# Normalising attention probabilities before the value matmul, with v as the stationary operand

## What is computed

```
q = l2norm((xn @ w_q) per head) * q_scale;  k the same;  v = xn @ w_v
k, v = concat(null_k, k), concat(null_v, v)             # 2 null keys and 256 keys
sim  = 8 * q @ k.T + distance * slope, causal
attn = softmax(sim, axis=-1)
out  = (attn @ v) gathered over the heads @ w_out
```

## Time and profile before

| | us |
|---|---|
| runs | 723.68, 727.42, 747.17; median 727.42 |
| profiled execution | 723.42, its span 721.6 |
| PE / DVE / ACT / POOL busy | 594.1 / 409.7 / 435.5 / 319.5 |
| granted TensorE clock, mean | 0.904 of full speed |

### The profile page before, as it was taken

How to read it: one execution, slowest core, us unless ns; L and a number is a source line. 1 busy time by engine, 2 the same in 40 slices (tenths; PEclk the granted TensorE clock), 3 DMA queues, 4 the chain that set the end, 5 groups by cost and what they waited for, 6 DMA issues and landing times.

```text
span 721.6 us, 12802 instructions
## 1 busy us (share of the span) xinstructions
PE 594.1 (82%) x3695; PEld 465.9 (65%) x3695; DVE 409.7 (57%) x1540; ACT 435.5 (60%) x1184; POOL 319.5 (44%) x281
## 2 busy tenths in 40 slices
PE   2467499914167689898999899999999999999997
PEld 2456388802046468566677667867787787777675
DVE  7546165523346463688446466647655764765574
ACT  1745466502156456766757587678768776876652
POOL 4477700035566632234677724404421441335770
PEclk9999699966577599979959999999999999999789
DMA  9611223241001000010111000000000000000220
GB/s 330 226 49 44 74 74 94 62 145 29 15 16 29 16 1 0 17 43 1 34 44 48 10 12 24 23 24 23 24 23 23 23 23 23 24 13 12 74 76 24
DMA packets 33074, 33.72 MB, mean 47 GB/s; under 512 B 4512, under 2 KB 28992, under 8 KB 32240
## 3 DMA queue, kind: packets, MB, share of 16 engines
q1 hardware_dynamic: 28912, 24.52, 10.8%
q0 software_dynamic: 4096, 8.40, 4.0%
HBM read 19.85 MB, written 13.04 MB: 46 GB/s over the span
## 4 chain that ended last, share of the span: by engine, by line
PE 43%; POOL 12%; DVE 9%; issue 5%; ACT 3%; DMA 1%; DVEq 0%; POOLq 0%; ACTq 0%
PE b_last L1737 8%; PE b_upB L1694 8%; PE b_rest L1718 4%; POOL sorted_rows L511 4%; POOL rn L570 3%; POOL taken L620 2%; PE b_upA L1656 2%; PE b_upB L1543 2%; PE b_upB L1682 2%; PE b_rest L1706 2%; PE b_upB L1577 2%; PE b_last L1388 2%; POOL qk L313 1%; PE b_rest L1682 1%; POOL taken L542 1%
## 5 line engine op out<-in xcount | busy, mean ns | idle before, releaser
L570 POOL TENSOR_TENSOR rn<-ss,halves 128x8 f32<-128x8 f32 x64 | 105.2, 1643 | 248.0 <-DVE ss L1264 240.0
L841 ACT ACTIVATE prb<-prb,mneg 128x130 f32<-128x130 f32 (+1 forms) x256 | 114.8, 449 | 73.5 <-DVE mneg L1331 72.0
L1331 DVE CUSTOM_DVE_ANT_0 prb<-b_upB,bias 128x130 f32<-128x130 f32 (+1 forms) x256 | 83.0, 357 | 92.1 <-PE b_upB L1694 90.8
L1737 PEld LDWEIGHTS b_last<-v,prT 128*128 128x128 f32 x768 | 106.7, 204 | 24.9 <-DVE qs_all L1319 12.2
L1737 PE MATMUL b_last<-v,prT 128*128 128x64 f32 x768 | 111.5, 284 | 9.0 <-DVE qs_all L1319 8.9
L1694 PE MATMUL b_upB<-qkT 64*128 64x258 f32 (+1 forms) x512 | 98.0, 412 | 6.6 <-DVE mneg L1331 4.7
L852 ACT ACTIVATE prT<-b_rest 128x512 f32<-128x512 f32 (+1 forms) x128 | 62.0, 484 | 33.1 <-PE b_rest L1718 30.2
L511 POOL DMA_INDIRECT sorted_rows<-xf_all,pos x64 | 66.0, 1031 | 27.5 <-issue 18.8
L1694 PEld LDWEIGHTS b_upB<-qkT 64*128 64x128 f32 x512 | 49.6, 206 | 37.6 <-issue 19.4
L1718 PE MATMUL b_rest<-cst,prb 128*128 128x128 f32 x384 | 69.4, 292 | 0.6 <-ACT prb L841 0.3
L776 ACT ACTIVATE sq<-qk 128x512 f32<-128x512 f32 x64 | 40.3, 630 | 43.3 <-DVE ss L1262 41.3
(11 more groups left out here) (301 smaller groups left out, 1301.2 us busy)
## 6 DMA issues: line engine op xcount, KB each, us to landing
moe_buf<-sorted_rows SPq DMA_DIRECT2D x20, 128.0 KB, 2.5
expert_rows<-moe_buf SPq DMA_DIRECT2D x20, 128.0 KB, 1.8
moe_buf<-sorted_rows SPq DMA_DIRECT2D x39, 64.0 KB, 1.9
expert_rows<-moe_buf SPq DMA_DIRECT2D x39, 64.0 KB, 1.5
sorted_rows<-v SPq DMA_DIRECT2D x2, 1024.0 KB, 6.8
bias<-w_up SPq DMA_DIRECT2D x1, 2048.0 KB, 13.2
down<-w_dn SPq DMA_DIRECT2D x2, 1024.0 KB, 9.1
moe_buf<-w_up SPq DMA_DIRECT2D x4, 512.0 KB, 3.8
```

The lines of the kernel that those rows point to most:

```text
L570: nc.gpsimd.tensor_tensor(rn[hs], ss[hs], halves[:], ALU.pow).then_inc(*pool_f1(f"root{n}"))
L841: nc.scalar.activation(prb[p % 3][:, i, 0:n], prb[p % 3][:, i, 0:n], ACT.Exp, scale=-1.0, bias=mneg[:, qt, h:h + 1], accum_out=lsum[:, qt, ...
L1331: nc.vector.tensor_tensor_reduce(prb[p % 3][:, i, 0:n], b_sim[i][:, 0:n], bias[:, h, KEYS - n:KEYS], 1.0, FMAX, ALU.add, ALU.min, mneg[:, ...
L1737: ins = nc.tensor.matmul(b_pv[:, at:at + DH1], prT[p3 % 3][:, i, c * P:(c + 1) * P], v[:, c, h * DH1:(h + 1) * DH1], start=(p3 % 4 == 0 an ...
```

## The change

The probabilities themselves are now normalised, on DVE, in `prb`: in each step two reciprocals (one instruction) and two multiplications of 130 or 258 columns, ahead of the copy of the null columns. `turned_values` turns them in step p-2 instead of p-1, behind the wait for this normalisation, and `values` follows four steps behind instead of three. There v is the stationary operand (64 columns) and `prT` the moving one (128 columns): head A writes partitions 0 to 63 of `b_pv`, head B partitions 64 to 127, and a half's values lie there already turned. The null part becomes four matmuls of 128 columns, one step later. DVE copies `b_pv` straight to `oT`, first in step 8, 12, 16 and 20. The product with the sums (`o_half`), the four turns of each half and the eight-wide reciprocal go.

```diff
--- before.py
+++ after.py
@@ -335,22 +335,20 @@
             out += [f"op{h}" for h in outputs_at(p)] + [f"simB{p}"] * (p < STEPS)
-            out += [f"oT{h}" for h in halves_at(p, 8)]
-            out += [f"pv{p - 3}"] * (3 <= p < STEPS + 3)
-            out += [f"pvn{h}" for h in halves_at(p, 6)]
-            return out + [f"prT{p - 1}"] * (1 <= p <= STEPS)
+            out += [f"pv{p - 4}"] * (4 <= p < STEPS + 4)
+            out += [f"pvn{h}" for h in halves_at(p, 7)]
+            return out + [f"prT{p - 2}"] * (2 <= p < STEPS + 2)
         def dve_head_steps(p):
-            out = [x for h in halves_at(p, 7) for x in (f"rl{h}", f"norm{h}")]
+            out = [f"oT{h}" for h in halves_at(p, 8)]
             if p < STEPS:
...
             out += [x for h in halves_at(p, 5) for x in (f"pnh{h}", f"pnT{h}")] + [f"add{h}" for h in outputs_at(p)]
-            out += [f"null{p - 1}"] * (1 <= p <= STEPS)
-            return out + [f"oT{h}" for h in halves_at(p, 8)]
+            return out + [x for x in (f"rl{p - 1}", f"norm{p - 1}", f"null{p - 1}") if 1 <= p <= STEPS]
...
             out = [f"exp{ab}{p}" for ab in "AB"] if p < STEPS else []
-            return out + [f"prT{p - 1}"] * (1 <= p <= STEPS)
+            return out + [f"prT{p - 2}"] * (2 <= p < STEPS + 2)
@@ -843,14 +841,14 @@
             def values(b, p):
-                if 1 <= p <= STEPS:
-                    p1 = p - 1
-                    n1 = P * (p1 // HP + 1)
...
+                if 2 <= p < STEPS + 2:
+                    p2 = p - 2
+                    n2 = P * (p2 // HP + 1)
...
@@ -1307,17 +1305,11 @@
                 n = NULL + P * (qt + 1)
-                for half in halves_at(p, 7):
-                    tile, first = half // 2, half % 2 * HALF
-                    dve.wait_ge(*act_heads.at(b, f"expB{4 * half + 3}"))
-                    heads8 = rl[:, tile, first:first + HALF]
-                    nc.vector.reciprocal(heads8, lsum[:, tile, first:first + HALF]).then_inc(*dve_heads(f"rl{half}"))
-                    dve.wait_ge(*dve_heads.at(b, f"rl{half}"))
+                for half in halves_at(p, 8):
                     dve.wait_ge(*pe_heads.at(b, f"pvn{half}"))
-                    dve.wait_ge(*(pe_heads.at(b, f"oT{half - 2}") if half >= 2 else pe_heads.at(b - 1, f"oT{half + 2}")))
-                    nc.vector.tensor_tensor(o_half[half % 2].rearrange("p (h d) -> p h d", h=HALF), b_pv.rearrange("p (h d) -> p h d", h=HALF),
-                                            heads8.unsqueeze(2).to_broadcast([P, HALF, DH1]), ALU.mult).then_inc(*dve_heads(f"norm{half}"))
+                    dve.wait_ge(*(pe_heads.at(b, f"op{half - 1}") if half else pe_heads.at(b - 1, f"op{STEPS // 4 - 1}")))
+                    nc.vector.tensor_copy(oT[:].rearrange("p a q -> p (a q)"), b_pv).then_inc(*dve_heads(f"oT{half}"))
                 if p < STEPS:
@@ -1354,7 +1346,15 @@
                     half, at = p1 // 4, p1 % 4 * 2 * NULL
+                    q1, h1, n1 = p1 // HP, 2 * (p1 % HP), NULL + P * (p1 // HP + 1)
                     dve.wait_ge(*act_heads.at(b, f"expB{p1}"))
+                    nc.vector.reciprocal(rl[:, q1, h1:h1 + 2], lsum[:, q1, h1:h1 + 2]).then_inc(*dve_heads(f"rl{p1}"))
+                    dve.wait_ge(*dve_heads.at(b, f"rl{p1}"))
+                    for i in range(2):
+                        part = prb[p1 % 3][:, i, 0:n1]
+                        ins = nc.vector.tensor_scalar(part, part, rl[:, q1, h1 + i:h1 + i + 1], None, ALU.mult)
+                    ins.then_inc(*dve_heads(f"norm{p1}"))
+                    dve.wait_ge(*dve_heads.at(b, f"norm{p1}"))
                     if half >= 2:
@@ -1363,11 +1363,6 @@
                                           prb[p1 % 3][:, :, 0:NULL].unsqueeze(1).to_broadcast([P, 3, 2, NULL])).then_inc(*dve_heads(f"null{p1}"))
-                for half in halves_at(p, 8):
-                    dve.wait_ge(*pe_heads.at(b, f"oT{half}"))
-                    dve.wait_ge(*(pe_heads.at(b, f"op{half - 1}") if half else pe_heads.at(b - 1, f"op{STEPS // 4 - 1}")))
-                    nc.vector.tensor_copy(oT[:].rearrange("p a q -> p (a q)"), b_turned[half]).then_inc(*dve_heads(f"oT{half}"))
@@ -1609,8 +1604,6 @@
                     pe.wait_ge(tile_loaded[i % 4], 16 * (i // 4 + 1))
-                    for half in halves_at(p - 1, 8):
-                        pe.wait_ge(*dve_heads.at(b, f"oT{half}"))
@@ -1664,7 +1657,7 @@
                     pe.wait_ge(*dve_heads.at(b, f"null{4 * half + 3}"))
-                    pe.wait_ge(*(dve_heads.at(b, f"simA{p - 1}") if p <= STEPS else act_heads.at(b, f"prT{STEPS - 1}")))
+                    pe.wait_ge(*(dve_heads.at(b, f"simA{p - 1}") if p <= STEPS else act_heads.at(b, f"prT{STEPS - 2}")))
                     nc.tensor.transpose(b_null[half], pn3[half % 2][:], ident).then_inc(*pe_heads(f"pnT{half}"))
@@ -1676,8 +1669,8 @@
                             pe.wait_ge(*dve_heads.at(b, f"simB{p - 1}"))
-                        elif half == 2:
-                            pe.wait_ge(*dve_heads.at(b, "pnT3"))
+                        else:
+                            pe.wait_ge(*(act_heads.at(b, f"prT{STEPS - 1}") if half == 2 else dve_heads.at(b, "add2")))
@@ -1693,58 +1686,48 @@
-                for half in halves_at(p, 8):
-                    pe.wait_ge(*dve_heads.at(b, f"norm{half}"))
-                    if p < ROUND - 2:
-                        pe.wait_ge(*(dve_heads.at(b, f"oT{half - 1}") if half else dve_heads.at(b - 1, "oT2")))
-                        for i in tile_at(b, p - 1, 0):
-                            pe.wait_ge(tile_dve["xl"], i + 1)
-                    else:
-                        pe.wait_ge(*dve_heads.at(b, "add2"))
-                    for i in range(4):
-                        ins = nc.tensor.transpose(b_turned[half][:, i * P:(i + 1) * P], o_half[half % 2][:, i * P:(i + 1) * P], ident)
-                    ins.then_inc(*pe_heads(f"oT{half}"))
             def turned_values(b, p):
-                if 1 <= p <= STEPS:
-                    p1 = p - 1
-                    nc1 = p1 // HP + 1
-                    pe.wait_ge(*(act_heads.at(b, f"prT{p1 - 1}") if p1 else dve_heads.at(b - 1, "add3")))
-                    pe.wait_ge(*act_heads.at(b, f"expB{p1}"))
+                if 2 <= p < STEPS + 2:
+                    p2 = p - 2
+                    nc2 = p2 // HP + 1
+                    pe.wait_ge(*(act_heads.at(b, f"prT{p2 - 1}") if p2 else dve_heads.at(b - 1, "add3")))
+                    pe.wait_ge(*dve_heads.at(b, f"norm{p2}"))
+                    if p2 == STEPS - 1:
+                        pe.wait_ge(*dve_heads.at(b, "pnT3"))
                     for i in range(2):
...
             def values(b, p):
-                if 3 <= p < STEPS + 3:
-                    p3 = p - 3
-                    q3 = p3 // HP
-                    if p3 % 4 == 0:
-                        pe.wait_ge(*(dve_heads.at(b, f"norm{p3 // 4 - 1}") if p3 else dve_heads.at(b - 1, f"norm{STEPS // 4 - 1}")))
-                    if p3 == 0:
+                if 4 <= p < STEPS + 4:
+                    p4 = p - 4
+                    if p4 % 4 == 0:
+                        pe.wait_ge(*(dve_heads.at(b, f"oT{p4 // 4 - 1}") if p4 else dve_heads.at(b - 1, f"oT{STEPS // 4 - 1}")))
+                    if p4 == 0:
                         pe.wait_ge(*act_f1.at(b, "v3"))
-                    pe.wait_ge(*act_heads.at(b, f"prT{p3}"))
-                    for i in range(2):
-                        h = 2 * (p3 % HP) + i
-                        at = (p3 % 4 * 2 + i) * DH1
-                        for c in range(q3 + 1):
-                            ins = nc.tensor.matmul(b_pv[:, at:at + DH1], prT[p3 % 3][:, i, c * P:(c + 1) * P], v[:, c, h * DH1:(h + 1) * DH1],
-                                                   start=(p3 % 4 == 0 and i == 0 and c == 0), stop=False, skip_group_check=True)
-                    ins.then_inc(*pe_heads(f"pv{p3}"))
-                for half in halves_at(p, 6):
+                    pe.wait_ge(*act_heads.at(b, f"prT{p4}"))
+                    at = p4 % 4 * P
+                    for c in range(p4 // HP + 1):
+                        for i in range(2):
+                            h = 2 * (p4 % HP) + i
+                            ins = nc.tensor.matmul(b_pv[i * DH1:(i + 1) * DH1, at:at + P], v[:, c, h * DH1:(h + 1) * DH1],
+                                                   prT[p4 % 3][:, i, c * P:(c + 1) * P], start=(p4 % 4 == 0 and c == 0),
+                                                   stop=False, skip_group_check=True)
+                    ins.then_inc(*pe_heads(f"pv{p4}"))
+                for half in halves_at(p, 7):
                     if b == 0 and half == 0:
...
                     pe.wait_ge(*dve_heads.at(b, f"pnT{half}"))
-                    nc.tensor.matmul(b_pv, pnT[:], nvbd[:, half % 2], start=False, stop=True, skip_group_check=True)\
-                        .then_inc(*pe_heads(f"pvn{half}"))
+                    for i in range(4):
```

(3 more changed lines are left out.)

18 lines of the change are left out of this document (9 added, 9 removed).

## The result

The changed kernel took 793.07 us (median of 4 runs, 788.40 to 796.42) against 726.25 us for the kernel before (4 runs): a ratio of 1.093, interval 1.083 to 1.102. The forecast was 750 us, its range 718 to 772. The direction was right, the size was 2.5 times too small (66 us lost between the profiled executions, where 27 were forecast), and the time lies outside the range.

What follows compares the result with a forecast made beforehand. The prediction took PE to be the bound (busy 64.89 of 65.80 us in the sixth round) and summed 723.4 - 14 - 6 + 11 + 29 + 7 = 750 us, range 718 to 772.

Steps and rivals of the forecast that it cites:

- The turns, the values and the null part: On PE: dropped turns -14 us, values with two heads side by side -6, null part in four matmuls +11.
- The rival in which column pairs need nothing around them: Groups of values on PE cost their passes alone, 130 columns under 0.27 us; 700 us in all, chance 0.09.
- The wait for the copy: PE's first values of a half wait for DVE's copy to oT at steps 8, 12, 16: +29 us.
- The failed step: DVE normalisation, 0.75 or 0.87 us a step: free while DVE idles, but moves its lag.
- Rounds without tiles: Part of the wait for the copy to oT: +8 us in three rounds, +1 in the last.
- Column halves that do not run together: Both heads write the same bank, so values groups take 0.64 and 1.07 us; about 783 us, chance 0.06.
- slow multiplications: DVE's normalising multiplications at their slow end, about 0.25 us more a step; 762 us, chance 0.08.
- The rival of waits half as long: Waits half as long and pairs a little cheaper, so no change: 728 us, chance 0.27.
- The waits near the end of a round: Product with w_out and ACT's first copy of v wait, 0.4 and 0.5 us each: +7 us, between 0 and 14.

Runs made afterwards that it cites:

- no_norm: Changed kernel without the normalisation's reciprocals and multiplications, timetable kept (turns at two steps, values at four): 743.8 us, ratio 1.021 to the kernel before.
- the added turns: Changed kernel plus unread identity turns on PE in rounds 0, 1, 7 (two: 1.085) or 0, 1, 2, 7 (two: 1.057; four: 1.067), ratios to the kernel before.
- early_no_norm: Changed kernel without the normalisation, in the timetable of the kernel before (turns at one step, values at three): ratio 0.968 to the kernel before.
- values_early_no_norm: Changed kernel without the normalisation, turns kept at two steps, values at three and the copy to oT a step earlier: 775 and 759 us in two runs.
- sums_spread: early_no_norm plus reciprocals of eight sums, spread to 512 columns by a DVE copy, turned on PE, multiplied on the way to oT: ratio 0.988 to the kernel before.

## Why the prediction was wrong

The sign and the mechanism it named were right, the size was not.

- **The turns, the values and the null part** (-14, -6, +11). Together -9, or -1.1 us a round; measured -2.0 (65.8 to 63.8). Column halves run together (as the row halves of the earlier trace rows do) and their groups are shorter than forecast, by 0.06 and 0.05 us; the null part cost 0.18 instead of 0.34. The rival in which column pairs need nothing around them did not hold: 0.37 is over its 0.27. The Trainium skill (TensorEngine Tiling (Array Packing), Performance Considerations) recommends the swap for up to twice the speed; the groups of 0.40 and 0.84 us became 0.37 and 0.59, a gain of 8% and 30%.
- **The wait for the copy** (+29). Forecast about 20 places with 20 to 30 us; measured 20 with 24.1. But 8.9 us of such waits stood in the kernel before, which the sum did not set against it: this term was 15, and the total hit its number by luck. The places differ too: rounds 3 to 6 have 13 us where 20 were forecast, the others 11 where 9 were. In the steady round 1.8, 1.5 and 2.3 us were worked out; the starts in steps 8 and 12 are late by about 1.0 and 1.1, and the third wait is 1.5. The likely reason is that PE itself comes later to each, behind waits that were not in the sum.
- **The failed step** is "It costs nothing by itself while DVE has idle time, but it moves DVE's lag". The price was right: from the reciprocal to the null copy DVE needs 0.72 us in a step of 130 columns and 0.85 in one of 258, where 0.75 and 0.87 were forecast. But the lag was charged at three places of a round, those of the new wait. The normalisation alone costs 4.9 us of the steady round, of which the sum held some 2.5; and it costs 2.7 in the kernel before, which does not have the new wait. PE meets DVE's queue at every even step (the tile's hidden values, the null columns), not only there, and 24 us of idle time a round were no cover: DVE is idle because PE has not delivered yet, and what is then added comes in front of the instruction for which PE waits.
- **DVE and POOL.** The two longest pairs of multiplications a round lose 0.8 us each to a product of POOL. The forecast had POOL nowhere.
- **Rounds without tiles** (+8 for three rounds, +1 for the last). They lost 39 of the 66 us. In round 1 DVE also does the second layer's routing, and was busy for 46.4 of 63.0 us before; the forecast looked at a round for its steady state and carried its idle time over. Nor did the sum have a term for the clock, whose mean fell from 0.904 to 0.858. Round 1 of the changed kernel, cut to four stretches of 5 us:

```profile
310.00:315.00 5.00, 4.98 (x25) 3.14 (x23) 4.34 (x27) 4.41 (x16) 0.00 (x0) 0.65 0.01 3
...
325.00:330.00 5.00, 5.00 (x22) 2.66 (x21) 4.32 (x19) 2.53 (x8) 2.25 (x2) 0.50 0.04 15
...
345.00:350.00 5.00, 4.11 (x33) 2.84 (x32) 4.80 (x15) 3.41 (x10) 2.81 (x2) 0.94 0.00 2
...
355.00:360.00 5.00, 4.24 (x29) 2.32 (x27) 4.86 (x15) 2.12 (x6) 2.75 (x2) 1.00 0.00 2
```

 In the first two, at a low clock, PE is full and DVE (third of the engines) close behind; in the last two, with the clock back, DVE is the fuller one. Other stretches differ (from 350 to 355 PE has 4.97 us and DVE 3.54), so that no one engine bounds the round from end to end. How the 39 us divide is only partly settled. Without the normalisation the same rounds took some 25 us less (rounds 0, 1, 2 and 7 of `no_norm`: 72.4, 72.0, 60.4 and 58.6 to the end of the span, 263 against 289 us; on different chips, so roughly), and the added turns gave 9 to 11. The clock does not follow from the waits alone: `no_norm` ran round 1 at 0.74 with 7.5 us of waits of PE in its list, the kernel before at 0.89 with 6.4. What took the clock down in these rounds stays open.
- **The other rivals.** Column halves that do not run together, and slow multiplications, did not occur: two instructions are under way at one instant, as shown above, and a multiplication takes 0.28 to 0.36 us undisturbed. The rival of waits half as long came true for the one wait, and the time still went the other way.
- **The waits near the end of a round** (+7). The new wait for ACT's copy is there, 4.9 us in eight places (0.6 each, where 0.4 was forecast). The turns' step of delay costs 0.8 us of the steady round, which would make 6 to 7 in all; what it costs in the other rounds is not shown. `early_no_norm` ran round 1 in 58.5 us at 0.94 and `values_early_no_norm` in 70.1 at 0.73, but `sums_spread`, which has no such delay, took 71.1 at 0.78 on the chip of the latter.

The range was too narrow because every bound in it was a bound on a price, and none was on the number of places where a lag of DVE is met, or on the clock.

## What to carry to other kernels

An engine that is a third idle on average can still be the one that others wait for: before work is added to it, mark each point in a step at which another engine waits for it, and charge the addition at all of them. Look at the fullest round, not at the steady one. Where a normalisation (or another factor per row) must be moved, move it where it can be prepared ahead of the data: turning the factors instead of the data kept some of PE's gain here (`sums_spread`, 1.2% ahead of the kernel before).

## What the runs showed of the hardware that was not expected

- Of two multiplications in SBUF with a scalar per partition on DVE, the second, started 0.01 us behind a product of POOL in SBUF, ended only 0.09 us after it: 1.33 us for the pair instead of 0.48. The Trainium skill (SBUF — State Buffer, SBUF: two separate sides) states an exclusive lock between DVE in a two-port mode and GpSimd, held for a whole instruction; by that, the trace agrees.
- A reciprocal of 512 columns on DVE took 3.35 us, a copy of as many 0.43 us; of 8 columns it took 0.20 us and of 2 columns 0.16. Taken of the few and spread by the copy it is 5 times cheaper.
- From chip to chip the kernel before took 726 to 791 us (medians). The changed kernel took 793 and 849 us on two chips with a steady round of 72.05 and 72.06 us on them; on the slower one its first round began 24 us later, and round 2 took 82.3 us at a clock of 0.73 instead of 58.9 at 0.97.
